# An adaLN block on one core: two layer normalisations of the attention loop move from VectorE to ScalarE, with the bias made by GpSimd

## What is computed

```python
def _layernorm(x, axis=-1, eps=1e-05):
    m = jnp.mean(x, axis=axis, keepdims=True)
    v = jnp.var(x, axis=axis, keepdims=True)
    return (x - m) / jnp.sqrt(v + eps)
...
h = _layernorm(x, axis=-1) * (1 + ca) + sa
x = x + ga * _L0_attn_ref(h, L0_attn_Wqkv, L0_attn_bqkv, L0_attn_Wout, L0_attn_bout)
h = _layernorm(x, axis=-1) * (1 + cb) + sb
x = x + gb * _L0_ffn_ref(h, L0_ffn_router_w, L0_ffn_gate_up_proj, L0_ffn_down_proj, ...)
```

## Time and profile before

| | before |
|---|---|
| timed executions | 460.45, 463.87, 464.77 us (median 463.87) |
| profiled execution | 461.35 us; span of its instructions 459.6 us |
| TensorE clock granted, mean over the span | 0.979 |
| TensorE busy | 398.2 us, 3009 matrix instructions |
| VectorE busy | 313.6 us, 635 instructions |
| ScalarE busy | 227.7 us, 408 instructions |
| GpSimd busy | 212.8 us, 251 instructions |

### The profile page before, as it was taken

The page is one execution under the profiler, slowest core; times in us unless marked ns, Lnnn a source line. Parts: engine busy times, 40 slices in busy tenths (PEclk is TensorE's granted clock), DMA queues, the critical chain, the costliest instruction groups (busy, mean ns, idle before and its releaser), DMA issues.

```text
span 459.6 us, 8603 instructions
## 1 busy us (share of the span) xinstructions
PE 398.2 (87%) x3009; PEld 224.8 (49%) x3009; DVE 313.6 (68%) x635; ACT 227.7 (50%) x408; POOL 212.8 (46%) x251
## 2 busy tenths in 40 slices
PE   3789986598989899878989799999879999999991
PEld 3244542243554356434435264575555666666660
DVE  7678597268999898799968864879553434444441
ACT  2445556288584867547865746263213333232320
POOL 2395954343336963177354653101601555555342
PEclk9999999699999999999999999999999999999997
DMA  8547489359692578734357004992700444333210
GB/s 270 165 117 159 166 218 230 118 186 276 243 252 83 170 206 265 210 118 138 96 172 232 1 20 166 397 350 77 227 24 25 84 87 82 83 72 82 26 21 0
DMA packets 46192, 67.96 MB, mean 148 GB/s; under 512 B 5380, under 2 KB 33668, under 8 KB 46152
## 3 DMA queue, kind: packets, MB, share of 16 engines
q1 hardware_dynamic: 31064, 36.74, 27.4%
q10 hardware_dynamic: 9936, 22.55, 15.1%
q0 software_dynamic: 5152, 8.14, 9.0%
HBM read 43.14 MB, written 25.18 MB: 149 GB/s over the span
## 4 chain that ended last, share of the span: by engine, by line
PE 51%; DVE 18%; DMA 9%; ACT 7%; issue 5%; SPq 4%; POOL 3%; ACTq 1%; DVEq 0%; POOLq 0%
PE bank L1513 35%; DVE mx L1146 4%; DMA qk_d<-W 4%; DMA ng_d<-negm 4%; PE bank L1669 3%; PE bank L1653 3%; PE bank L1894 2%; SPq L541 2%; DVE rowg L1247 2%; ACT W L896 2%; PE bank L1624 2%; PE bank L1601 1%; DVE W L1247 1%; DVE x_sb L1191 1%; PE bank L1528 1%
## 5 line engine op out<-in xcount | busy, mean ns | idle before, releaser
L896 ACT ACTIVATE W<-bank 128x512 f32<-128x512 f32 (+1 forms) x176 | 93.7, 562 | 61.6 <-PE bank L1653 43.5
L1146 DVE TENSOR_REDUCE mx<-bank 128x1 f32<-128x384 f32 (+3 forms) x176 | 104.9, 632 | 27.4 <-PE bank L1626 24.0
L1513 PE MATMUL bank<-W 128*128 128x256 f16 (+2 forms) x756 | 103.9, 289 | 5.3 <-DVE x_sb L1191 1.7
L1513 PEld LDWEIGHTS bank<-W 128*128 128x128 f16 x756 | 72.7, 99 | 38.1 <-issue 8.5
L768 POOL TENSOR_SCALAR_AFFINE_SELECT W<-W 128x512 f32<-128x512 f32 x64 | 47.8, 748 | 83.9 <-ACT W L896 83.9
L1653 PE MATMUL bank<-W 128*128 128x512 f16 (+3 forms) x256 | 63.3, 304 | 18.9 <-ACT W L896 9.7
L1513 PE MATMUL bank<-W,h2T 128*128 x276 | 67.3, 380 | 2.8 <-DVE W L1262 2.0
L839 POOL DMA_INDIRECT out<-h2T,sidx x23 | 36.3, 1578 | 67.5 <-DVE h2T L1483 67.1
L1624 PE MATMUL bank<-W 126*128 126x128 f16 (+3 forms) x208 | 52.5, 304 | 5.6 <-DVE mx L1146 4.2
L1669 PE MATMUL bank<-W 128*32 128x128 f32 (+3 forms) x512 | 48.6, 454 | 0.8 <-POOL W L768 0.8
L1653 PEld LDWEIGHTS bank<-W 128*128 128x128 f16 x256 | 21.3, 97 | 55.6 <-ACT W L896 29.2
(11 more groups left out here) (173 smaller groups left out, 558.8 us busy)
## 6 DMA issues: line engine op xcount, KB each, us to landing
w_d<-rowg ACTq DMA_DIRECT2D x18, 512.0 KB, 3.7
W<-w_d SPq DMA_DIRECT2D x18, 512.0 KB, 7.9
stage<-in_gup ACTq DMA_DIRECT2D x14, 512.0 KB
qk_d<-W SPq DMA_DIRECT2D x48, 128.0 KB
W<-qk_d SPq DMA_DIRECT2D x32, 192.0 KB, 5.1
stage<-in_down ACTq DMA_DIRECT2D x7, 512.0 KB
x_sb<-in_x SPq DMA_DIRECT2D x4, 512.0 KB, 9.5
h_d<-gbb SPq DMA_DIRECT2D x4, 512.0 KB, 4.6
```

Of the source, the lines that this page charges most:

```text
L896: a.activation(PT[j][:, i:i + m, :], t_bank(N)[:, 0:m * w].rearrange("p (i n) -> p i n", i=m), ACT.Exp).then_inc(s_exp, 1)
L1146: v.tensor_reduce(mx_v[:, b % 2, hp0 // 4, par, i:i + m, t], s_bank(N)[:, 0:m * w].rearrange("p (i n) -> p i n", i=m), AX.X, ALU.max).then ...
L1513: i = t_.matmul(outp, l, r, start=(n == 0), stop=(n == len(prods) - 1), **kw)
```

## The change

`norm1` (in the loop) and `scale2` leave VectorE. ScalarE does them at the same slots as one activation of kind Identity a tile: x * root + (-mean * root), with root and product as columns. GpSimd's `rstd` makes the product, two more instructions on 128x4 each time, each after a wait on the one before, and only then raises the semaphore. `rstd` of batches 0 and 1 in the head and of the last batch's second norm makes none. VectorE's wait for its own variance (`s_mv2`) goes with it. On TensorE and SyncE nothing moves.

```diff
--- before.py
+++ after.py
@@ -195,6 +195,8 @@
         mv1 = sb("mv1", [P, NT, 2])
         ve1 = sb("ve1", [P, NT])
         rs1 = sb("rs1", [P, NT])
+        mr1 = sb("mr1", [P, NT])
+        mr2 = sb("mr2", [P, NT])
         st2 = sb("st2", [P, NT, 6])
         mv2 = sb("mv2", [P, NT, 2])
         ve2 = sb("ve2", [P, NT])
@@ -708,12 +710,18 @@
                 link(g.tensor_copy(it[:, :], it_i[:, :]))
                 g.tensor_scalar(itp[:, :], it[:, :], float(P), 0.0, ALU.mult, ALU.add).then_inc(s_const, 1)
 
-            def rstd(ve, mv, rs, b, ready, done):
+            def rstd(ve, mv, rs, mr, b, ready, done):
 
                 c = slice(TT * b, TT * (b + 1))
                 po.wait_ge(ready, b + 1)
                 link(g.tensor_scalar(ve[:, c], mv[:, c, 1], EPS, 0.0, ALU.add, ALU.add))
-                g.tensor_tensor(rs[:, c], ve[:, c], neghalf[:, :], ALU.pow).then_inc(done, 1)
+                root = g.tensor_tensor(rs[:, c], ve[:, c], neghalf[:, :], ALU.pow)
+                if mr is None:
+                    root.then_inc(done, 1)
+                    return
+                link(root)
+                link(g.tensor_tensor(mr[:, c], mv[:, c, 0], rs[:, c], ALU.mult))
+                g.tensor_scalar(mr[:, c], mr[:, c], -1.0, 0.0, ALU.mult, ALU.add).then_inc(done, 1)
 
             def modulation_rows(part):
 
@@ -783,11 +791,11 @@
                     po.wait_ge(s_h2w, 16 * b)
                 g.tensor_scalar(h2s[:, t], h2f[:, t], srow[:, n:n + 1], 0.0, ALU.mult, ALU.add).then_inc(s_rows, 1)
 
-            rstd(ve1, mv1, rs1, 0, s_mv, s_rstd)
+            rstd(ve1, mv1, rs1, None, 0, s_mv, s_rstd)
             mask_constants()
             h_low(0, 0)
             h_low(0, 1)
-            rstd(ve1, mv1, rs1, 1, s_mv, s_rstd)
+            rstd(ve1, mv1, rs1, None, 1, s_mv, s_rstd)
             for u in range(4):
                 qk_low(0, u)
             for b in range(-1, B):
@@ -800,13 +808,13 @@
                         mask(NG * b + n // UNITS, CUM.index(n % UNITS + 1))
                     for job, c, k in gpsimd_jobs(b, n):
                         if job == "stats1":
-                            rstd(ve1, mv1, rs1, c, s_mv, s_rstd)
+                            rstd(ve1, mv1, rs1, mr1, c, s_mv, s_rstd)
                         elif job == "turn":
                             h_low(c, k)
                         elif job == "qk":
                             qk_low(c, k)
                         elif job == "stats2":
-                            rstd(ve2, mv2, rs2, c, s_mv2, s_rstd2)
+                            rstd(ve2, mv2, rs2, mr2, c, s_mv2, s_rstd2)
                         elif job == "scale2":
                             modulate2(c, k)
                         elif job == "bias":
@@ -816,7 +824,7 @@
                             rows(c, 2 * k + 1)
             for t in range(TT):
                 rows(B - 2, t)
-            rstd(ve2, mv2, rs2, B - 1, s_mv2, s_rstd2)
+            rstd(ve2, mv2, rs2, None, B - 1, s_mv2, s_rstd2)
 
             def gather(r):
 
@@ -885,6 +893,24 @@
                     a.activation(dst, side_bank("qk", b, u)[:, :], ACT.Identity,
                                  bias=bqk[:, 2 * isk + u // 2:2 * isk + u // 2 + 1],
                                  scale=1.0 / WS if isk else 0.25 / WS).then_inc(s, 1)
+
+            def norm1(b):
+                ac.wait_ge(s_rstd, b + 1)
+                if b:
+                    ac.wait_ge(s_xt, KC * b)
+                for t in range(TT):
+                    n = TT * b + t
+                    a.activation(xn[:, t], x_sb[:, n], ACT.Identity, bias=mr1[:, n:n + 1],
+                                 scale=rs1[:, n:n + 1]).then_inc(s_xn, 1)
+
+            def scale2(b, t):
+                n = TT * b + t
+                ac.wait_ge(s_rstd2, b + 1)
+                if t == 0 and b:
+                    ac.wait_ge(s_ht, KC * b)
+                    ac.wait_ge(s_rows, TT * b)
+                a.activation(h2f[:, t], x_sb[:, n], ACT.Identity, bias=mr2[:, n:n + 1],
+                             scale=rs2[:, n:n + 1]).then_inc(s_hm, 1)
 
             def exps(N):
                 G, n = N // UNITS, N % UNITS
@@ -1003,7 +1029,11 @@
                     if n % UNITS == 4 and G > 0:
                         outs(G - 1)
                     for job, c, k in side_jobs(b, n):
-                        if job == "turn":
+                        if job == "norm1":
+                            norm1(c)
+                        elif job == "scale2":
+                            scale2(c, k)
+                        elif job == "turn":
                             h_parts(c, k)
                         elif job == "qk":
                             qk_parts(c, k)
@@ -1198,13 +1228,6 @@
                 for t in range(TT):
                     i = v.bn_aggr(mv2[:, TT * b + t], st2[:, TT * b + t])
                 i.then_inc(s_mv2, 1)
-
-            def scale2(b, t):
-                n = TT * b + t
-                ve.wait_ge(s_mv2, b + 1)
-                ve.wait_ge(s_rstd2, b + 1)
-                v.tensor_scalar(h2f[:, t], x_sb[:, n], mv2[:, n, 0:1], rs2[:, n:n + 1],
-                                ALU.subtract, ALU.mult).then_inc(s_hm, 1)
 
             def centre2(b):
 
@@ -1341,16 +1364,12 @@
                             v_out(c, k)
                         elif job == "stats1":
                             stats1(c)
-                        elif job == "norm1":
-                            norm1(c)
                         elif job == "attn":
                             attn_low(c, k)
                         elif job == "out":
                             residual(c, k)
                         elif job == "stats2":
                             stats2(c)
-                        elif job == "scale2":
-                            scale2(c, k)
                         elif job == "h2":
                             h2_low(c, k)
                         elif job == "score":
```

## The result

Four executions of the changed kernel took 464.56, 464.20, 467.01 and 468.42 us, median 465.78; four of the kernel before on the same chip 464.77, 463.87, 460.45 and 458.15, median 462.16. The ratio is 1.0122 with a 95% interval of 1.0074 to 1.017: the kernel became 1.2% slower, which is 5.6 us of 462.16 (3.4 to 7.9). The two medians are only 3.6 apart (0.8%), and the spans of the two profiled executions 3.2 (462.8 after, 459.6 before). Executions over 1.5% above the fastest of the same kernel are left out of every ratio in this document.

The account below looks back on a forecast made before the run. TensorE bounds the kernel, stalled when ScalarE or VectorE empties score banks late. 2.1 + 0.5 + 1.05 + 0.5 = +4.2 us on 462.6, the middle of four executions, gives 466.8 us; 8-in-10 range 461 to 471.

Parts of the forecast that it names:

- a fall of the clock in batch 1 or 2: Sign against the prediction: it is wrong if TensorE's clock falls in either of these batches of the loop; no size given.
- Price of the instruction: The new ScalarE norm instruction takes 586 ns, between 497 and 685, costing ScalarE about 0.5 us each in a row.
- GpSimd's pair: The added multiply and negation on GpSimd's 128x4 tiles delay the bias by 0.64 us, or 1.45 if slow.
- Batch 1: Slots 25 to 31: ScalarE waits for the bias and TensorE gets the whole delay, +2.1 us, bounds 1.5 and 3.
- Batch 2: From slot 25: exps(26) starts 3.2 us later, mostly absorbed by TensorE's waits for maxima; net +0.5 us, ends -1.2 and +3.2.
- rival C: TensorE's clock drops once or twice more in the loop, +1.7 us each, 468.5 to 470.2 us; chance 0.15.
- Batch 3: From exps(26): it moves +2.9 us, an idle 2.13 before exps(28) goes; net +1.05 us, ends 0 and +2.9.
- norm1: Block before slot 11 of batch 1 costs +0.5 us for batch 3's norms, ends 0 and +2.0; 0 for batch 2's.
- Behind the loop: Everything after the loop is a chain on TensorE that moves as it is, no further gain or loss.
- A: Faster through VectorE's relief: four TensorE waits in batches 1 to 3 go, -4.4 us, 458.2 us; chance 0.12.
- B: No change: slots behind each delay catch up in the loop, within 2 us of before, 462.6 us; chance 0.16.
- D: Nothing is absorbed in the loop: every delay reaches the end, +10.2 us, 472.8 us; chance 0.07.

Follow-up runs that it names:

- filler: The changed kernel plus unread TensorE matmuls before slot 28's transposed score, ten in batch 1 and six in batch 2; ratio 1.0065 to the kernel before.
- wait_only: The kernel before, both norms still on VectorE, but GpSimd makes the second norm's product and ScalarE only waits for it at scale2's slots; ratio 1.0083.
- scale2_only: The kernel before with only scale2 moved to ScalarE (twelve instructions), norm1 staying on VectorE; ratio 1.0126.
- norm1_only: The kernel before with only norm1 moved to ScalarE (eight instructions), scale2 staying on VectorE and its product not made; ratio 0.997.
- placebo: The kernel before plus an unused scratch tile and one start-up wait of ScalarE for bias rows long landed, no work added; ratio 1.003.
- work_only: The kernel before plus twelve ScalarE activations of the same form at scale2's slots, on always-ready data, results unread; ratio 1.0075.
- after_again: The changed kernel measured once more, unaltered, beside its variants; ratio 1.0134 to the kernel before.
- late1: The changed kernel with scale2's four slots one later (26, 28, 30, 32) on all engines; ratio 1.0123 to the kernel before.
- late2: The changed kernel with scale2 two slots later (27, 29, 31, 33); ratio 1.0166 to the kernel before.
- work_again: The kernel before plus twelve unread, always-ready ScalarE activations at scale2's slots, the same program measured a second time with 11 executions; ratio 0.9977.

## Why the prediction came out

The median, 465.78, is 1.0 below the forecast of 466.8, and the forecast +4.2 lies within the 3.4 to 7.9 us of the ratio. The path was the one forecast: ScalarE waits for GpSimd's product and hands the wait to TensorE. What the sum left out was the clock. The prediction had named a fall of the clock in batch 1 or 2 as a sign of being wrong, and it fell in both; by that sign of its own the account was incomplete, though the number came out. That the number is so near is partly luck: the loop cost 6.1 us, not 4.2, and the medians moved by 3.6.

- **Price of the instruction: right.** 604 and 588 ns in the mean against 586. The other bounds, 497 and 685, were not needed. The estimate from the Trainium skill (ScalarE: Activation LUTs, What ACT_TABLE_LOAD costs; the prediction names the section behind it), 585 ns, agrees with the 588 ns of L903.
- **GpSimd's pair: 0.55 instead of 0.64.** 0.20 and 0.19 with gaps of 0.07 and 0.09 before them. The multiply is plain arithmetic and nothing like the power (1.04).
- **Batch 1, forecast +2.1: the wait gave 2.0, right to 0.1** (`exps(26)`; the whole stage is 1.8 in `filler`). It splits into 1.5 of wait (`wait_only`) and 0.5 of norm. But the stage cost 3.0, since the clock fell after it: +0.9 more from slot 28 to slot 30, absent in `filler`.
- **Batch 2, forecast +0.5, came out at +2.0: the mis-sized term.** The walk through the slots was sound: without a clock drop the stage is −0.2 (`filler`), inside the +0.5 with its bounds; `wait_only` has +0.6 with the 0.57 from 212 to 216 in it. The missing piece was the clock at 1.2 GHz for all of 208 to 212, some 2 us, by the difference of `filler` and the kernel after. This is rival C, which I priced at 1.7 a drop and held as an alternative with 0.15, though it followed the forecast's own wait in all three profiles that have it unfilled in batch 1. It was an addition to the forecast and belonged in its sum: +0.9 and +2.2, 3.1 for two.
- **Batch 3, +1.05 forecast, +0.8 measured**, and 0.8 and 0.7 in `scale2_only` and `filler`. Right; these four profiles, the kernel before among them, all have a stretch of low clock there.
- **norm1, +0.5 forecast, +0.6 measured** in the profiles after, of `norm1_only` and of `filler`; the block for batch 2 in front of the wait of 7.8 us cost nothing, as said.
- **Behind the loop, "moves as it is": wrong by 2.3 us.** The kernel before had a long wait in its tail that no other profiled execution has. Timeline of TensorE before, then after:

```profile
332.98 1.47 PE L1513 MATMUL bank<-W,h2T 128*128 x6 [2.00 <-DVE W L1262]
336.13 5.41 PE L1513 MATMUL bank<-W 128*128 128x256 f16 x48 [1.69 <-DVE W L1270]
```

```profile
338.65 5.41 PE L1532 MATMUL bank<-W 128*128 128x256 f16 x48 [0.94 <-DVE W L1293]
```

   The first wait is missing after, the second is 0.94 instead of 1.69. All eleven experiments, `placebo` with the kernel before's own work among them, also show 0.93 or 0.94 and no 2.00. So 2.75 us (2.00 + 1.69 − 0.94) belong to the one profiled execution before, and are no gift of the change. I had taken its tail as a constant; one execution can't show that. It hid what the clock took: the slots add up to +6.1 (0.6 + 3.0 + 2.0 + 0.8 is 6.4, less 0.3 given back in between), the span to +3.2. The ratio's 5.6 us side with the slots.
- **Rivals.** A (relief of VectorE) fell: of its four waits the 0.67 shrank to 0.48, one 1.28 stayed, and the two of 1.23 became 1.46 and 2.05; `work_only` shows that ScalarE's idle time is free, but the condition of A was that the bias be ready in time, and it is not. What A added on VectorE and GpSimd slowing each other came to little: GpSimd's factor went from 856 to 956 ns and its offset from 975 to 759, 1.4 us less in all over 24 instructions. B (catching up) fell: of batch 1's 3.0 only 0.3 is given back before slot 25 of batch 2. D fell: `exps(26)` of batch 2 was +3.2 late and batch 3's +2.8, as D says, but within three slots 3.0 and 1.7 of these were absorbed. C happened, beside the forecast.

What remains open: what decides the clock drop: it followed the 2.6 us of batch 1 in all three profiles that had them (after, `after_again`, `scale2_only`) and 1.16 in `late1`, but not 2.12 in `wait_only`, and in slots 16 to 19 of batch 2 it came behind a wait of 1.27 or 1.28 us in `placebo`, `norm1_only`, `after_again` and `late1`, but not in the kernel after, `scale2_only`, `work_only`, `late2` or `filler` behind the same wait, nor behind 2.26 us in `work_again`; what set off the wait in the tail of the kernel before; and whether a product made on VectorE, or a root asked for earlier, would take the wait away. None of these was tried. No version here beat the kernel before: `norm1_only`, 0.997 [0.991, 1.003], cannot be told from it.

## What to carry to other kernels

An engine with idle time can take work for nothing only if the operand is there when the engine comes; twelve activations cost 0, and one wait in front of them cost 1.5 us, because an engine in order passes a wait on to everything behind it. So compare the time at which the new producer is done with the time at which the new consumer arrives, and then look for the chain on its other side: here the same norm two slots later hit GpSimd's chain instead. When a forecast makes TensorE wait, put the clock drop that may follow into the sum (1 to 2 us each here), and do not file it as another outcome. Where the same profile is compared slot by slot, look first whether the baseline's own execution had the clock up.

## What the runs showed of the hardware

- TensorE's clock drops to 1.2 GHz even where it is not idle throughout: in batch 2 two waits of 1.28 and 1.46 us with matmuls between them were followed by 0.50 from 208 to 212. It does not follow every wait: `work_again` waited 2.26 us until 194.77, was busy 1.62 of 4 us from 192 to 196, and kept 1.00.
- Matmuls whose result nobody reads can pay: with 16 of them, 2.33 us for ten, the mean granted clock of the span went from 0.969 back to 0.978, and the ratio from 1.0122 and 1.0134 to 1.0065.
- The transfer of the maxima lands anywhere within 4 us at the start of batch 1: TensorE waited 0.24 us for it before, 0.49 after, and up to 4.10 in the experiments; the same program had 3.70 (`work_only`) and 2.01 (`work_again`). At the 4.10 the DMA engines were full; from the busy times by stretch of `wait_only`:

```profile
112.00:116.00 4.00, 1.51 (x16) 0.54 (x14) 1.86 (x4) 2.24 (x3) 1.27 (x2) 1.00 1.05 348
116.00:120.00 4.00, 2.39 (x10) 1.17 (x10) 0.69 (x1) 1.06 (x2) 0.00 (x0) 0.58 0.67 248
```

   A DMA share of 1.05 (before, 0.92 in the same stretch), and a clock of 0.58 from 116 to 120. I take this for a good part of the spread of one kernel (before: 457 to 468 us), which was not tested apart; it is why a ratio under 1% needs the shifts by slot beside it.
- The 128x4 multiply on GpSimd takes 0.20 us, the power on the same shape 1.04.
